# Seven output stores of a row-tiled cross network: nine transfers of every ninth row in place of one transfer of 128 rows

## What is computed

```
x0 = inputs                       # [16384, 4096] float32
x = x0
for wi, bi in zip(w, b):          # 6 layers, wi [4096, 1], bi [4096]
    xw = x @ wi                   # [16384, 1]
    x = x0 * xw + bi + x
return x
```

## Time and profile before

| what | value |
|---|---|
| three executions | 1281.05 us median (1280.29 to 1283.19) |
| profiled execution, its own time | 1280.2 us |
| its span, first to last instruction | 1278.4 us |
| outside the span | 1.8 us |
| DVE busy | 1150.2 us, 90% of the span |
| PE busy | 780.7 us, 61% |
| ACT busy | 102.7 us, 8% |
| bytes moved | 537.28 MB, 420 GB/s over the span |

### The profile page before, as it was taken

The page is one execution under the profiler, slowest core; times in us unless marked ns, Lnnn a source line. Parts: engine busy times, 40 slices in busy tenths (PEclk is TensorE's granted clock), DMA queues, the critical chain, the costliest instruction groups (busy, mean ns, idle before and its releaser), DMA issues.

```text
span 1278.4 us, 20057 instructions
## 1 busy us (share of the span) xinstructions
PE 780.7 (61%) x9114; PEld 728.6 (57%) x9114; DVE 1150.2 (90%) x526; ACT 102.7 (8%) x345; POOL 4.3 (0%) x17
## 2 busy tenths in 40 slices
PE   8666666555656655556555665665655665665653
PEld 4666566555556655555545565565655654665653
DVE  5999999898988988989889898898998988989896
ACT  3000000000000000000000000000000000000010
POOL 1000000000000000000000000000000000000000
PEclk9877787887877778778787777777777778678677
DMA  9999999999999999999999999999999999999996
GB/s 385 416 380 428 430 431 431 429 427 429 433 429 431 431 430 432 430 431 424 421 424 425 418 427 421 424 425 422 427 424 421 424 423 425 425 423 425 426 421 286
DMA packets 37385, 537.28 MB, mean 420 GB/s; under 512 B 4168, under 2 KB 4168, under 8 KB 4728
## 3 DMA queue, kind: packets, MB, share of 16 engines
q1 hardware_dynamic: 18432, 268.44, 50.1%
q10 hardware_dynamic: 18936, 268.64, 49.3%
HBM read 268.63 MB, written 268.44 MB: 420 GB/s over the span
## 4 chain that ended last, share of the span: by engine, by line
DMA 72%; DVE 15%; PE 8%; issue 3%; ACT 1%; DVEq 0%
DMA out_dram<-tiles 56%; DMA tiles<-in_r_inputs_dram 15%; DVE tiles L286 8%; DVE blocks L264 7%; PE dots L401 6%; ACT spread L197 1%; PE dots L359 1%; PE scratch L339 1%; DMA tiles<-in_L_rec_w_dram 0%; PE strips L334 0%; PE strips L349 0%; ACT c_last L189 0%; PE turned L370 0%; DVE scale L275 0%; DVEq L42 0%
## 5 line engine op out<-in xcount | busy, mean ns | idle before, releaser
L401 PE MATMUL dots<-blocks,weights 128*64 128x128 f32 x7808 | 662.6, 349 | 380.8 <-DVE blocks L264 380.6
L401 PEld LDWEIGHTS dots<-blocks,weights 128*64 128x64 f32 x7808 | 628.7, 185 | 405.3 <-DVE blocks L264 405.2
L264 DVE STREAM_TRANSPOSE blocks<-tiles 128x2048 f32<-128x2048 f32 x256 | 576.0, 2288 | 100.1 <-issue 100.1
L286 DVE SCALAR_TENSOR_TENSOR tiles<-tiles,scale,c_last 128x4096 f32<-128x4096 f32 (+1 forms) x131 | 571.9, 4368 | 0.2
L197 ACT ACTIVATE spread<-dots,group_mask 128x128 f32<-128x128 f32 (+1 forms) x268 | 75.2, 363 | 1062.6 <-PE dots L401 1020.3
L370 PE MATMUL turned<-layer_sel,spread 128*128 128x8 f32 x512 | 68.1, 258 | 85.5 <-ACT spread L197 85.5
L370 PEld LDWEIGHTS turned<-layer_sel,spread 128*128 128x128 f32 x512 | 62.3, 191 | 101.4 <-issue 95.6
L359 PE MATMUL dots<-blocks,weights 128*64 128x64 f32 x768 | 32.4, 266 | 11.0 <-DVE blocks L264 11.0
L359 PEld LDWEIGHTS dots<-blocks,weights 128*64 128x64 f32 x768 | 31.7, 180 | 12.9 <-issue 12.9
L205 ACT ACTIVATE growth<-turned,ones 128x16 f32<-128x16 f32 (+1 forms) x67 | 18.3, 273 | 85.0 <-PE turned L370 85.0
L275 DVE TENSOR_TENSOR_SCAN scale<-growth,cw 128x6 f32<-128x6 f32 x128 | 13.3, 142 | 8.9 <-ACT growth L205 8.9
(11 more groups left out here) (25 smaller groups left out, 11.3 us busy)
## 6 DMA issues: line engine op xcount, KB each, us to landing
tiles<-in_r_inputs_dram SPq DMA_DIRECT2D x128, 2048.0 KB, 14.9
out_dram<-tiles ACTq DMA_DIRECT2D x127, 2048.0 KB, 25.5
out_dram<-tiles ACTq DMA_DIRECT2D x4, 512.0 KB, 7.0
tiles<-in_L_rec_w_dram ACTq DMA_DIRECT2D x1, 96.0 KB
tiles<-in_L_rec_b_dram ACTq DMA_DIRECT2D x1, 96.0 KB
```

Of the source, the lines that this page charges most:

```text
L264: nc.vector.transpose(blocks[:, p % PLACES, :], source).then_inc(blocks_ready, 1)
L286: nc.vector.scalar_tensor_tensor(out=tiles[:, s, at], in0=tiles[:, s, at], scalar=scale[:, u % 2, t, L - 1:L], in1=c_last[:, at], op0=ALU. ...
L401: last = nc.tensor.matmul(dots[at:at + KM * Q, :, :, :], weights[:, c * CH // Q + k:c * CH // Q + k + KM, :], place[:, :, k * Q:(k + KM) * Q],
```

## The change

`spared(n)` picks the tiles with n % 17 == 9 among those that `store` handles: 9, 26, 43, 60, 77, 94 and 111. Their stores are issued as nine transfers instead of one. Transfer r takes the rows r, r + 9, r + 18 and so on of the tile, in SBUF as in memory: 15 rows for r = 0 and 1, and 14 rows for r = 2 to 8, together the same 128 rows. Each of the nine adds 16 to the place's semaphore. `stored_by(n)` sums what the semaphore must have reached, and SP's wait at L142 and ACT's waits at the end use it. Nothing else differs: the loads, the computation and the other 121 stores are as before.

```diff
--- before.py
+++ after.py
@@ -18,6 +18,8 @@
 N_SLOTS = 8
 HEAD, TAIL = 2, 4
 PIECES = 4
+STEP = 9
+EVERY, FIRST = 17, 9
 
 
 def cross_network(nc, x, w, b, out):
@@ -26,7 +28,6 @@
     n_tiles = rows // P
     n_pairs = (n_tiles - HEAD - TAIL) // TB
     n_units = HEAD + n_pairs + TAIL
-    n_rounds = n_tiles // N_SLOTS
     PIECE = D // 2
     CH = PIECE // TB
     STRIPS = L * G
@@ -128,6 +129,12 @@
             turned_rows = w_turned[rows, :].rearrange("p (k q) -> p k q", q=Q)
             return into, turned_rows[:, :, 0:STRIPS].rearrange("p k (l j) -> p j l k", j=G)
 
+        def spared(n):
+            return n % EVERY == FIRST
+
+        def stored_by(n):
+            return sum(16 * STEP if spared(m) else 16 for m in range(n % N_SLOTS, n + 1, N_SLOTS))
+
         @block.sync
         def _(sp):
             for s in range(N_SLOTS):
@@ -138,7 +145,7 @@
                 sp.dma_start(tiles[:, s, :], x[s * P:(s + 1) * P, :]).then_inc(x_landed[s], 16)
             for n in range(N_SLOTS, n_tiles):
                 s = n % N_SLOTS
-                sp.wait_ge(y_stored[s], n // N_SLOTS * 16)
+                sp.wait_ge(y_stored[s], stored_by(n - N_SLOTS))
                 sp.dma_start(tiles[:, s, :], x[n * P:(n + 1) * P, :]).then_inc(x_landed[s], 16)
 
         @block.gpsimd
@@ -206,8 +213,14 @@
                                      bias=ones[:, 0:1]).then_inc(growth_ready, 1)
 
             def store(n):
+                s = n % N_SLOTS
                 act.wait_ge(tiles_done, n + 1)
-                act.dma_start(out[n * P:(n + 1) * P, :], tiles[:, n % N_SLOTS, :]).then_inc(y_stored[n % N_SLOTS], 16)
+                if spared(n):
+                    for r in range(STEP):
+                        act.dma_start(out[n * P + r:(n + 1) * P:STEP, :],
+                                      tiles[r:P:STEP, s, :]).then_inc(y_stored[s], 16)
+                else:
+                    act.dma_start(out[n * P:(n + 1) * P, :], tiles[:, s, :]).then_inc(y_stored[s], 16)
 
             keep_bias(0)
             spread_dots(0)
@@ -236,7 +249,7 @@
                 act.dma_start(out[n * P:(n + 1) * P, at], tiles[:, n % N_SLOTS, at]).then_inc(y_stored[n % N_SLOTS], 16)
             for s in range(N_SLOTS):
                 last_stores = 1 if s < N_SLOTS - 1 else PIECES
-                act.wait_ge(y_stored[s], 16 * (n_rounds - 1 + last_stores))
+                act.wait_ge(y_stored[s], stored_by(n_tiles - N_SLOTS + s) + 16 * (last_stores - 1))
 
         @block.vector
         def _(dve):
```

## The result

The kernel got slower: 1297.48 us median of six runs (1293.09 to 1301.70) against 1280.95 us (1280.11 to 1283.19), **16.5 us more**, a ratio of 1.0128 with a 95% interval of 1.0105 to 1.0151. The forecast was 1285.4 us, range 1264 to 1289 us: the direction was right, the size was a quarter of what came, and the range missed it. The profiled execution took 1295.78 us, 1.7 us under that median. (Two groups of rows ahead of the prediction stand in exchanged places: what it cites as rows 10, the first loads, is printed as rows 11, and the other way round; from here on the printed numbers are used.)

A forecast was written before the change was run, and what follows sets the result against it. One slow DMA engine was taken to bound the kernel. Seven extra rows on it, 4.3 us, with all else at zero, took 1280.2 to 1284.5 us, or 1285.4 us on the median's scale; range 1264 to 1289 us.

The forecast's parts named there:

- The bound: DMA queues: one of 16 engines is slower, 0.619 us a row against 0.609, and sets the kernel's pace from 200 us on.
- How the rows fall on the engines: Seven divided stores: one row per engine, same leading engines each time; 14 get nine rows, one two, one none, not eight.
- the forecast's case: Divided stores: the slow engine is among the 14 that take transfers of 14 rows; 1285.4 us, chance 0.62.
- Rival A: Divided stores: the slow engine is left out of the transfers of 14 rows and spared 56 rows; 1265 us, chance 0.25.
- Rival B: Divided stores: each transfer begins at another engine, all get about eight rows; no change, 1281 us, chance 0.08.
- The division of the store at zero: Nine transfers per spared tile: more completions, ACT's issues, the start of the engines and SP's wait each priced at 0.
- the ninth row: Each of seven divided stores costs the slow engine one more row, 7 x 0.619 = 4.3 us, delaying the loads that follow.
- the further completions: Stores' queue: 56 more completions for each of 14 engines, taken as zero, upper end 0.05 us each, 2.8 us.
- the engines' start: Divided stores: the ninth transfer leaves 2.7 us later or more, but the slow engine's backlog keeps it from running dry; 0.
- The forecast's cover: Odd spared tiles on ACT: 4.9 us before DVE's scan needs the growth instruction hides 2.7 to 5.7 us of issues; 0.
- The signs named beforehand: Changed profile: loads 9.9 us apart, one 10.5 after each spared tile, 424 GB/s late, 25 GB/s stretches in tail, 19720 packets.
- Rival C: Divided stores: short transfers are dear and hold up the spared store; 1292 us, up to 1323 us, chance 0.05.

## Why the prediction was partly right and mostly wrong

**The bound: right.** One DMA engine sets the pace: its completion comes 11.2 to 14.0 us behind the fifteenth. More work for the DMA engines costs time (9.9 us for 256 KB more in seven stores), while the work on ACT doesn't (held for 7 us: 1.0000).

**How the rows fall on the engines: right.** 19720 packets came, as worked out, and 126 rows gave 16 completions with two more. That the slow engine is among those that take the transfers of 14 rows was the forecast's case, and the late completions of the changed kernel show it. Rival A is refuted. Rival B, an even deal, doesn't fit the run with 112, 7, 5, 3 and 1 rows, where the same number of completions is late at five tiles.

**The division of the store at zero: wrong.** This is the step that failed. The sum has the ninth row and nothing else: it puts the further completions, the issues and the engines' start at zero. Measured, eight transfers without a ninth row cost 8 to 9 us where every engine keeps its own partitions (eight column pieces) and 20.8 us as every eighth row; a single further transfer from the same partitions costs 0.8 us in each store (column halves). The forecast's reason for the zero was misread too: of the 504 packets by which the stores' queue exceeds that of the loads only 72 are completions (4168 small packets in all, 2048 of them of the loads' queue), the rest is the last tile's and the weights' packets of 4 KB. A completion by itself is cheap all the same: its packet takes 9 ns in the trace, so 784 more of them are 7 us in all, spread over 16 engines. What else a further transfer costs the slow engine is not settled.

**The ninth row, 0.62 us each: perhaps too small.** The price was the pace of a load row and a store row side by side, 9.90 us over 16. Measured, 16 KB more in the stores' queue cost 1.0 us, 7.0 us for seven, with 0.5 to 1.6 us allowed by the intervals, and 9.9 us with the transfer that carried them. Even at 7 us the row is less than half of the loss. The forecast divided a time by a number of rows and took the quotient for the price of one more row of one kind; that a store row is dearer than the average is not shown.

**Which partitions an engine reads: not in the prediction at all.** Of the terms missing it is the largest that was isolated: with the same number of issues and completions eight transfers cost 8.9 us or 20.8 us, by the rows that they take. 126 and 2 rows cost 16.7 us with two transfers, where one row and one further transfer for every engine, from its own partitions, cost 9.9 us; the 6.8 us between them are left for the other partitions and for the uneven deal, and no run parts these two.

**Together:** 4 to 7 us for the rows, 3 to 6 us for dividing, the rest for who reads what, and perhaps 3 us for ACT. These are measured one at a time and are not a sum: added up they give more than 16.5 us.

**ACT: nearly right.** The forecast's cover (4.9 us) is there, and a hold of 7 us by itself is free. But the issues took 0.79 to 2.6 us each, beyond its upper price of 0.71 us, and one of DVE's waits for the growth instruction was 5.9 us.

**The signs named beforehand:** one load of 10.5 us after each spared tile was expected. In the trace the load that reuses the tile's place goes out 13.5 to 15.7 us after the one before it, and the next 6.1 to 7.1 us later. The 424 GB/s late in the run became 415. The packet count came as named, and so did the slices of one engine's rate in the tail (22 GB/s in slices of 0.75 us). Rival C, dear short transfers, was closest with its 1292 us, and it had 0.05: the evidence cited against it, the backlog of the slow engine, says that the engine never runs dry; it doesn't say that its work stays the same.

## What to carry to other kernels

Where one DMA engine sets the pace of a whole kernel, price a change of its transfers by a run with one more transfer of that kind, not by bytes over bandwidth: here 16 KB more for each engine came to some 1.0 us and a divided store to 0.7 us (four of 32 rows) up to 3.0 us (every eighth row). Keep large stores whole, 128 rows at once; if one must be divided, compare several ways to cut it, since ways with the same counts differed by 12 us. And use a busy share of DMA engines for nothing but a first look: it stayed at 1.00 while the rate fell to 256 GB/s.

## What the runs showed of the hardware that was not expected

- An issue of a transfer of 14 or 15 rows took ACT 0.79 us at least, over twice the 0.338 us of one of 128 rows, and up to 2.6 us late in a group of nine. The number of engines alone doesn't do it: the issues of 126 and of 2 neighbouring rows took 0.28 to 0.39 us.
- Transfers with equal bytes, issues and completions took different times by the rows they held: eight of 16 rows cost 20.8 us as every eighth row and 8.9 us as neighbouring rows, in seven stores.
- One of the sixteen DMA engines is behind all others: fifteen completions of a store came within 12.6 us of its issue, the last after 25.4 us. Completion packets took 9 ns each.
- One further transfer of 256 KB behind every seventeenth store changed the rhythm of all others: loads landed 17.4 us after their issue in place of 14.9 us, at a pace that stayed 9.9 us between the disturbed tiles.
